# Two-layer cross attention: the transposes of A and of the probabilities moved from TensorE to DRAM bounces and VectorE

## The reference

```python
Mn = Wn @ inorm(x) + bn;  Mm = Wm @ inorm(ctx) + bm          # 128 x 512 each
A  = softmax(Mn.T @ Mm)                                      # 512 x 512
x1 = Wo @ ((Wl @ ctx + bl) @ A.T) + bo + x                   # layer 0
q  = layer_norm(x1) @ q_w + q_b; k, v = ctx @ k_w + k_b, ctx @ v_w + v_b
P  = softmax(q k.T / sqrt(32))                               # 16 heads of 128 x 128
h  = (P v) @ cproj_w + cproj_b + x1
out = h + gelu(layer_norm(h) @ fc_w + fc_b) @ proj_w + proj_b   # 512 -> 2048 -> 512
```

## Time and profile before

| | |
|---|---|
| median of 3 runs | 3116.62 us (3113.08 to 3116.71) |
| the profiled execution | 3114.79 us |
| its span, first to last instruction | 3112.8 us |
| TensorE busy | 3043.9 us, 98% |
| VectorE, ScalarE, GpSimd busy | 1802.5, 1499.1, 796.0 us |
| DMA | 149.5 MB, mean 48 GB/s |
| end of the attention stage | about 1700 us of the span |

### The profile page before, as it was taken

One profiled execution on the slowest core, in us unless ns is written; L12 is line 12 of the kernel. 1 busy time (PEld: TensorE's weight loads), 2 busy tenths in 40 slices (PEclk: granted clock), 3 DMA queues, 4 the chain that ended last, 5 costly groups with the idle time before them and its releaser, 6 DMA issues. The chain is left out here.

```text
span 3112.8 us, 56124 instructions
## 1 busy us (share of the span) xinstructions
PE 3043.9 (98%) x19575; PEld 2582.9 (83%) x19575; DVE 1802.5 (58%) x3577; ACT 1499.1 (48%) x4210; POOL 796.0 (26%) x742
## 2 busy tenths in 40 slices
PE   6999999999999999999996999999999999999999
PEld 5888888888888888888885888888888888888887
DVE  6777777777777777777774433333333333333332
ACT  5777777777777777777774211111111111111111
POOL 4444444444444444444433100000000000000000
PEclk8999999999999999999998999999999999999999
DMA  4111111111111111111102211111110111111110
GB/s 129 45 52 56 52 52 52 52 53 55 52 52 52 52 52 52 52 52 56 58 32 81 85 31 38 40 40 40 40 40 14 40 35 33 40 40 40 40 27 14
DMA packets 232040, 149.49 MB, mean 48 GB/s; under 512 B 142912, under 2 KB 176192, under 8 KB 231872
## 3 DMA queue, kind: packets, MB, share of 16 engines
q1 hardware_dynamic: 231872, 146.91, 16.0%
HBM read 97.57 MB, written 33.55 MB: 42 GB/s over the span
## 5 line engine op out<-in xcount | busy, mean ns | idle before, releaser
L1218 ACT ACTIVATE gl<-pre,fc_bias 128x512 f32<-128x512 f32 x256 | 176.6, 690 | 1119.9 <-PE pre L1303 1119.9
L1257 DVE CAST hT_hi<-gl 128x512 fp32r<-128x512 f32 x256 | 109.1, 426 | 839.5 <-ACT gl L1218 839.5
L641 ACT ACTIVATE rows<-bank,negmax 128x128 f32<-128x128 f32 x1024 | 359.4, 404 | 10.2 <-DVE negmax L745 10.2
L1301 PE MATMUL pre<-yT_lo,rest_hi 128*128 128x512 f32 x768 | 298.8, 389 | 0.0
L1302 PE MATMUL pre<-yT_hi,rest_lo 128*128 128x512 f32 x768 | 298.8, 389 | 0.0
L1303 PE MATMUL pre<-yT_hi,rest_hi 128*128 128x512 f32 x768 | 298.8, 389 | 0.0
L1301 PE MATMUL acc<-rest_lo,hT_hi 128*128 128x512 f32 x768 | 298.8, 389 | 0.0
L1302 PE MATMUL acc<-rest_hi,hT_lo 128*128 128x512 f32 x768 | 298.8, 389 | 0.0
L1303 PE MATMUL acc<-rest_hi,hT_hi 128*128 128x512 f32 x768 | 298.8, 389 | 0.0
L567 POOL TENSOR_TENSOR rows<-rows,rsum 128x512 f32<-128x512 f32 x256 | 261.4, 1042 | 90.0 <-DVE rsum L741 89.2
L609 ACT ACTIVATE rows<-bank,negmax 128x512 f32<-128x512 f32 x256 | 175.0, 688 | 213.0 <-DVE negmax L762 213.0
(11 more groups left out here) (160 smaller groups left out, 7926.7 us busy)
## 6 DMA issues: line engine op xcount, KB each, us to landing
x_ctx_in<-in_x SPq DMA_DIRECT2D x64, 256.0 KB, 2.6
x_ctx_in<-in_ctx SPq DMA_DIRECT2D x64, 256.0 KB, 2.9
blocks<-in_ctx SPq DMA_DIRECT2D x256, 64.0 KB, 1.9
small<-in_x SPq DMA_DIRECT2D x64, 256.0 KB, 3.5
hidden<-hid SPq DMA_DIRECT2D x64, 256.0 KB, 2.0
rows<-hidden SPq DMA_DIRECT2D x16, 1024.0 KB, 5.5
out<-rows SPq DMA_DIRECT2D x64, 256.0 KB, 2.1
stage<-y SPq DMA_DIRECT2D x240, 64.0 KB, 2.1
```

The costliest lines, as they stand in the source:

```text
L641: act.activation(probs[:, r, c, :], by_chunk(S1_BANK[r])[:, c, :], ACT.Exp, bias=negmax1[:, r, c:c + 1], accum_out=sum1[:, r, c:c + 1]).th ...
L1218: act.activation(gl[:, i % 2, :], pre[i % 2][:], ACT.Gelu_apprx_tanh, bias=mlp.fc_bias[:, i:i + 1]).then_inc(gelu_done, 1)
L1301: pe.matmul(out, a_hi, b_lo, start=first, stop=False)
```

## The change

- **No more transposes of A and of the probabilities on TensorE**, and no copies of them out of PSUM. Scaled A is written by SP to a DRAM tensor `a_turn` (two DMAs of 512 KB), read back by four DMAs of 256 KB into 32 partitions each (pieces of 512 B), and turned by four VectorE transposes. The probabilities go the same way through `p_turn`: two writes of 512 KB in pieces of 1 KB, four reads of 256 KB in pieces of 2 KB, four VectorE transposes into `pT`.
- **A's lower halves** go from VectorE to GpSimd (four instructions); its upper halves are made out of SBUF.
- The first half of k or q is copied with its bias by ScalarE (two instructions of 256 columns), the second by VectorE (one).
- **Six batches in flight**: S1, the probabilities and their turning are for b4, all in one slot; PV, C and `hid` for b5; V and `x1n` for b2. The slots run to B + 4. The lists of all five engines are put in another order. `x_in`, `ctx_in` and `hid` lose their second buffer.

Core of the diff:

```diff
@@ VectorE, one slot: its new list (edits shown as what stands there now)
+   if b2: bn_aggr, x1_ve
+   wait s1_done(b4); maxima1(0); maxima1(1); x1n(b2); maxima1(2); maxima1(3)
+   sum1_reciprocal(0); outT_lo(b5); v_sb(b2); sum1_reciprocal(1); in_stats(ahead)
+   turn_A(0); xnT_lo(b2); sum1_reciprocal(2); turn_A(1); m_lo(b0) x2; turn_A(2); turn_A(3)
+   hid(b5); sum1_reciprocal(3); normed(ahead) x2; transpose of ctx; mask_less_1
+   maximum0(0..3); turn_probs(0); reciprocal of sum0; u_lo(b1); turn_probs(1..3)
+   second half of kT or qT; x1(b1); its bn_stats
```

```diff
@@ VectorE
+                def turn_probs(r):
+                    if b4.exists():
+                        if r == 0:
+                            dve.wait_ge(p_blocks_in, b4.nth(64, 64))
+                        dve.transpose(pT[:, r, :, :].rearrange("p c (q b) -> p c q b", b=32),
+                                      p_blocks[:, :, r * P:(r + 1) * P].rearrange("p q (c b) -> p c q b", b=32))\
+                           .then_inc(pT_set, 1)
+                def turn_A(c):
+                    if b1.exists():
+                        if c == 0:
+                            dve.wait_ge(a_blocks_in, b1.nth(64, 64))
+                        dve.transpose(A[:, c, :].rearrange("p (q b) -> p q b", b=32),
+                                      a_blocks[:, :, 32 * c:32 * (c + 1)]).then_inc(at_turned, 1)
@@ SP
+            def write_probs(e, half):
+                if half == 0 and e.has_before(1):
+                    after(pT_set, (e + -1).nth(4, 4))
+                after(probs_set, e.nth(4, 2 * half + 2))
+                cols = slice(256 * half, 256 * (half + 1))
+                sp.dma_start(p_turn[:, :, cols], probs_flat[:, :, cols]).then_inc(p_written, 16)
+            def read_probs(e):
+                after(p_written, e.nth(32, 32))
+                for d in range(4):
+                    sp.dma_start(p_blocks[32 * d:32 * (d + 1), :, :],
+                                 p_turn[:, d, :].rearrange("(q p) n -> p q n", p=32)).then_inc(p_blocks_in, 16)
...
             def slot(s):
+                    read_A(b1), after pT_set(b5) and a_written(b1)
...
+                    write_probs(b4, 0); store of hid(b5); write_probs(b4, 1)
+                    load of x and ctx (s + 2); read_probs(b4)
...
+                    load_blocks(s + 1); write_A(s)
@@ GpSimd, one slot: its new list
+   x1b(b2); x1_rstd(b2); ctxT_lo(b1); normalise(0); normalise(1); in_rstd(ahead)
+   normalise(2); normalise(3), each after rsum1_set(b4)
+   at_lo(b1) x4, each after at_hi_set; new on this engine
+   normed_lo(ahead) x2
@@ ScalarE, one slot: its new list
+   ctxT_hi(b1); exp1(0); outT_hi(b5); exp1(1); exp1(2); xnT_hi(b2); m_hi(b0) x2; exp1(3)
+   at_hi(b1) x4; normed_hi x2; first half of kT or qT (2)
+   exp0(b0) x4, each also after at_lo_set(b1, t + 1)
+   u_hi(b1); wait rsum0_set; scale A x4
@@ TensorE, one slot: its new list
+   S1(b4); PV(b5) after pT_set(b5, 4); V(b2); M(b0); x1n(b2); C(b5); QK first half
+   S0(b0); U(b1) after at_lo_set(b1, j + 1); QK second half; OUT0(b1) after u_lo
-                        turn(bank[AT_BANK[j]], lambda t: A[:, t, j * P:(j + 1) * P], at_turned)
-                        turn(bank[PT_BANK[r]], lambda c: probs[:, r, c, :], pT_turned)
```

More of the change, by code:

```diff
@@ L338, in attention_pass @@
         q_done = sem("q_done")
-        qT_set = sem("qT_set")
+        qT_set = [sem(f"qT_set{i}") for i in range(2)]
         k_done = sem("k_done")
-        kT_set = sem("kT_set")
+        kT_set = [sem(f"kT_set{i}") for i in range(2)]
         v_done = sem("v_done")
@@ L486, in slot @@
                     load_weight(C_W)
+                if (s + -4).exists():
+                    write_probs(s + -4, 0)
+                e = s + -5
+                if e.exists():
+                    after(hid_set, e.nth(1, 1))
+                    sp.dma_start(hidden[e.number], hid[:]).then_inc(hid_stored[e.parity], 16)
+                if (s + -4).exists():
+                    write_probs(s + -4, 1)
+                e = s + 2
+                if e.exists() and e.has_before(2):
+                    load(e)
+                if (s + -4).exists():
+                    if (s + -1).exists():
+                        after(at_turned, (s + -1).nth(4, 4))
+                    read_probs(s + -4)
                 e = s + 1
@@ L489, in slot @@
                     load_blocks(e)
[L490 to L493, removed]
+                if s.exists():
+                    write_A(s)
             def load_for_mlp():
@@ new lines, in slot @@
+                if ahead.exists():
+                    for i in range(2):
+                        act.wait_ge(normed_set, ahead.nth(2, i + 1))
+                        act.activation(normed_hi[:, i, :], normed[:, i, :], ACT.Copy).then_inc(normed_hi_set, 1)
+                if s.parity == 0 and b1.exists() and b2.exists():
+                    act.wait_ge(k_done, b2.pair_nth(2, 1))
+                    for c in range(2):
+                        act.activation(kT[:, b2.quarter // 2, c, :], bank[QK_BANK[0]][:, c * 2 * P:(c + 1) * 2 * P],
+                                       ACT.Identity, bias=vecs[:, 3, c:c + 1]).then_inc(kT_set[0], 1)
@@ L658, in slot @@
                     upper_halves(C_W)
[L660 to L668 removed]
+            slots(act, slot, {1: lambda: upper_halves(V_W), LAST - 2: lambda: first_weights(0)})
         @block.vector
@@ new lines, in slot @@
+                sum1_reciprocal(0)
+                if b5.exists():
+                    dve.wait_ge(outT_hi_set, b5.nth(1, 1))
+                    lower(flat(outT_lo), bank[PV_BANK][:], flat(outT_hi), outT_lo_set)
+                if b5.exists() and not b4.exists():
+                    first_group()
+                if b2.exists():
+                    dve.wait_ge(v_done, b2.nth(1, 1))
+                    if not b2.has_before(1):
+                        dve.wait_ge(vecs_in, 16 * 6)
+                    dve.tensor_tensor(v_sb[:, b2.quarter, :], bank[V_BANK][:], v_bias[:], ALU.add).then_inc(v_set, 1)
@@ L748, in slot @@
+                turn_A(0)
+                if b2.exists():
+                    dve.wait_ge(xnT_hi_set, b2.nth(1, 1))
+                    lower(pair_half(xnT_lo, b2), by_chunk(XN_BANK), pair_half(xnT_hi, b2), xnT_lo_set)
+                sum1_reciprocal(2)
+                turn_A(1)
                 if b0.exists():
@@ new lines, in slot @@
+                if b1.exists():
+                    if b0.exists():
+                        pe.wait_ge(m_lo_set, b0.nth(2, 2))
+                    pe.wait_ge(ctxT_lo_set, b1.nth(1, 1))
+                    for j in range(DC):
+                        pe.wait_ge(at_lo_set, b1.nth(4, j + 1))
+                        last = three_passes(bank[U_BANK][:], ctxT_hi[:, j, b1.parity, :], ctxT_lo[:, j, b1.parity, :],
+                                            at_hi[:, j, :], at_lo[:, j, :], j == 0, j == DC - 1)
+                    last.then_inc(u_done, 1)
```

566 lines of the change are left out of this document (285 added, 281 removed).

## The result

The changed kernel takes 3512.11 us (median of 4 runs, 3506.94 to 3515.33) against 3116.15 us of the kernel before: a ratio of 1.1271, with a 95% interval from 1.1252 to 1.1291. It is slower, as forecast, and 92 us above the forecast of 3420, inside the range. The profiled execution took 3512.02 us.

A forecast was written before the change was run, and what follows sets the result against it. The prediction took TensorE to bound the kernel before (25.2 us a slot) and loop 2 (30.0 us) after: 3114.8 + 288 for 60 slots + 15 at the end = 3418, forecast as 3420 us, range 3130 to 3600.

The forecast's parts named there:

- the bounce: Probabilities through DRAM, from the last scaling's end to turn_probs(0): 10.1 us, bounds 6.4 and some 12.
- The rival of full width: Bounce reads run at 400 GB/s: bounce 8.9 us, 3275 us in all; 25%.
- The 8.0 us: Bounce by the Trainium skill's rule of about 2.0 us plus bytes at 436 GB/s; would give 3166 us.
- the list's work: VectorE from turn_probs(0) to the next slot's sum1_reciprocal(3): 25 tile-size instructions and small ones, 16.8 us.
- loop 2: Slot-to-slot chain through A, with the bounces of the probabilities and of A: 30.0 us, said to set the slot.
- Loop 1: Slot-to-slot chain of VectorE's list, the last scaling and the probabilities' bounce: 28.0 us.
- TensorE's clock: Rival: the clock falls to half in idle time, VectorE waits some 4.5 us for V; slot 33 us, 3600 us; 15%.
- the ends: One more slot at the end, with one bounce exposed and PV and C behind it: +15 us.
- The clock of 0.50 in the slots: Sign in the changed profile's slots that would show the forecast wrong: granted clock at 0.50.
- Loop 3: Slot-to-slot chain without DMA, through GpSimd's last scaling and at_lo, U, half a projection and OUT0: 24.5 us.
- the full gain: Slot of 21.9 us with two groups of sixteen transposes off TensorE, saving 214 us; left out as forbidden.
- the faster rival: At the lower-bound bounce of 6.4 us the 24.5 us chain without DMA sets the slot: 3088 us; 12%.

The follow-up runs named there:

- Run 1: The changed kernel without the probabilities' DRAM bounce (no write to p_turn, no reads; turn_probs turns the tile in SBUF): 3141.93 us, ratio 1.0094 to the kernel before.
- run 7: The changed kernel with the four turn_probs moved behind x1 and its statistics, and PV between V and M: 3286.18 us, ratio 1.0550 to the kernel before.
- run 5: The changed kernel with the four reads of p_turn replaced by one 1 MB read into 128 partitions: 3396.38 us, ratio 1.0912 to the kernel before.
- Run 2: The changed kernel without A's DRAM bounce, turn_A(0) reading a block tile filled once: 3489.57 us, ratio 1.1211 to the kernel before.
- run 3: The changed kernel with 13 dummy matmuls on TensorE before OUT0 and 4 behind it: 3484.18 us, ratio 1.1194 to the kernel before.
- run 4: The changed kernel with dummy matmuls in TensorE's gaps and no DRAM bounce of A: 3404.12 us, ratio 1.0929 to the kernel before.
- run 8: The kernel before with A's bounce alone, the probabilities staying on TensorE and at_lo on VectorE: 3286.08 us, ratio 1.0552 to the kernel before.
- run 10: The changed kernel with turn_probs behind x1 and A's lower halves on VectorE before the maxima: 3351.06 us, ratio 1.0765 to the kernel before.

## Why the prediction was right, and where it was not

- **Right: what the change runs into.** A wait of 7 us inside VectorE's list, ended by DMA, at `turn_probs(0)`, with the whole next slot queued behind it. Predicted 5 to 8 us, measured 7.1. Run 1 takes the wait away, run 7 only moves it; both show it. The wait of 1 to 2 us before `turn_A(0)` that was forecast beside it isn't there.
- **Right: the bounce, within 9%.** 11.0 us in the mean against 10.1: writes 3.1 (3.0), reads done 7.6 us after the first issue (6.7), at 203 GB/s where 220 was taken from k_w. The rival of full width falls, and run 5 shows what it would have given. The 8.0 us that the prediction works out from the Trainium skill ("DMA: Bandwidth & Descriptors", section "Anatomy of one DMA") is 3 us short of the 11.0; that section's figures are for DMAs that GpSimd issues, and these are issued by SP. The Trainium skill ("SBUF — State Buffer", section "Door 1: The DMA port swizzle (why `[64,N]` ≈ `[32,N]`)") says that 32 partitions reach 8 of the 16 ports. Here the trace agrees: 203 GB/s at a share of 1.04, half of the 405 of the earlier trace rows.
- **Right: the list's work.** From `turn_probs(0)` to the last reciprocal the prediction counted 16.8 us; 938.13 - 918.28 = 19.85, less the waits for TensorE of 0.92 and 2.24, is 16.7, and the mean of 25 slots, 18.6 less 2.0, is the same.
- **Wrong: which loop.** "The slot is set by loop 2: 30.0 us". Run 2 refutes it: without A's bounce the slot stays at 31.0. Loop 2 was sized well (30.7 where it binds, run 3), but it was second. Loop 1, put at 28.0, measures 16.7 (list) + 2.0 (waits for S1 and V) + 1.5 (last scaling 1.25 instead of 1.04, with hand-overs) + 11.0 (bounce) = 31.2, against a mean slot of 31.12. The forecast of 3420 came as near as it did in part by luck: loop 1, put 3.1 us too low, lies only 1.1 us above the 30.0 of the wrong loop.
- **The step that failed** is that TensorE's clock was left out of loop 1 and stood as a rival only, with 15% and all or nothing: 4.5 us of waits. The fall did come, in every slot looked at; it cost 2.0 us, and without it (run 4) loop 1 is 29.6 us, below the 30.7 of loop 2. Only a part of V runs at half clock, since the clock is back before V ends. By the rival's own reasoning (idle time in few long gaps) it deserved the larger part of the chance, and the argument against it misread its row: the stretch at 0.50 in the earlier trace rows is 3.00 of 4.00 us busy, 75%, and 73% is not more. What the clock costs the kernel is less still: run 3 gives back 28 us, because loop 2 is just behind.
- **Mis-sized: the ends.** +15 us predicted, some 47 measured. The prediction had the extra slot at the end and nothing at the start, but the first `hid` comes 30.1 us late, 11 of it by A's bounce (run 2). The rest is at the end, where slots stay 24 to 31 us apart though their work is gone. That it is the bounce which they still pay was not tested. With 5.66 instead of 4.8 us a slot (351 instead of 288) that is the 92 us between forecast and result, within 3 us.
- **Signs.** TensorE busy 81%, not 73 to 78: at the half clock its work takes longer (25.3 us a slot, 22.9 in run 1). DMA share 0.64, within 0.55 to 0.65. The clock of 0.50 in the slots had been named as a sign that the forecast is wrong, and of its loop that holds.
- **Loop 3 was right in kind.** It was said to forbid the full gain, at 24.5 us. Run 1 measures 25.6 with 0.5 us of A's bounce in it, so even very short bounces would have left the faster rival (3088 us, 12%) almost nothing to gain: by these rows some 25.1 us a slot against 25.46, which no run tests. Missing in the 24.5 was what VectorE and GpSimd take from each other: 0.55 us in `x1n` and 0.2 in the last scaling. A slip in that rival: loop 1 falls under 25.2 us with a bounce under 7.3, not 7.1 (17.9 + 7.3); it changes nothing.

## What to carry to other kernels

Before work is taken off the busiest engine, write down what goes round from slot to slot on the others: a DMA round trip that is waited for within the slot, in an in-order list, adds to everything queued behind it what the work ahead of the wait doesn't cover (7.1 of 11.0 us here). A bounce of 1 MB through DRAM costs some 11 us here; its wait belongs where its data has long landed (run 7: -226 us with the same DMAs). And when one limit is removed and little comes back, look at once for the next one standing behind it: 28 and 22 us alone were 108 together (of the slot 0.4, 0.1 and 1.5).

## What the runs showed of the hardware

- A gap of 2.3 us (run 8) or 3.6 us (after) on TensorE, once a slot, was followed by a granted clock of 0.50: for some 7 us in run 8 (0.53 from 918 to 920 us, 0.77 from 924 to 926) and some 10 us after the change (0.81 from 918 to 919 us, 0.57 from 928 to 929). Filling the gap with matmuls of no use (run 3) brought the mean clock from 0.922 to 0.971.
- VectorE beside GpSimd. The lines of `normed` after the change, from 500 to 1300 us (min/median/max ns):

```profile
L892 DVE TENSOR_SCALAR x_ctx<-x_ctx,in_mv,in_rstd x52: 509/890/1270, 502.3 to 1281.3; 128x512 f32<-128x512 f32 x52
```

  The first of the two takes 0.51 us, the second 1.27, from 938.64 to 939.91, where GpSimd's last scaling ends at 939.62; the scaling, begun while the first `normed` ran, takes 1.25 instead of 1.04. `x1n` takes 1.10 instead of 0.54 when GpSimd's `ctxT_lo` runs beside it, `mask_less` 0.66 instead of 0.19, and a tensor_tensor with both inputs in SBUF 1.78 instead of 0.68 (run 10). Each time VectorE's instruction ended 0.25 to 0.55 us after GpSimd's. The Trainium skill ("SBUF — State Buffer", section "Who interferes with whom") has both forms contend for a shared port, the later one blocked until the first is done; these rows agree in kind. Such a wait shows as a longer instruction, not as idle time before it.
- Reads into groups of 32 partitions moved 196 to 250 GB/s at shares of 1.04 to 1.08 (914 to 917 us after the change), though four of them were under way at once, to four different groups.
